# Residual sum ahead of the second norm: two fused operations on VectorE in place of one on ScalarE and two on GpSimd

## The reference

```
x = x + tanh(g_xattn) * _L0_xattn_ref(_layernorm(x), ctx, ctx, ..., ln_scale)
...
h = einsum('hst,htd->hsd', C / (normalizer + EPS), vh)          # inside _L0_xattn_ref
return (h - mu) / sqrt(var + LN_EPS) * ln_scale
...
x = x + tanh(g_ffn) * _L0_ffn_ref(_layernorm(x), w1, w2, w3, ..., gate_weight, ...)
```

## Time and profile before

| | before |
|---|---|
| median of 3 runs | 826.05 us (825.72 to 828.82) |
| the profiled execution | 823.55 us, span of the profile 821.5 us |
| TensorE / VectorE busy | 686.1 us (84%) / 544.9 us (66%) |
| ScalarE / GpSimd busy | 374.5 us (46%) / 403.2 us (49%) |
| mean granted TensorE clock | 0.803 of full speed; near half of it in the attention stage |

### The profile page before, as it was taken

How to read it: one execution, slowest core, us unless ns; L and a number is a source line. 1 busy time by engine, 2 the same in 40 slices (tenths; PEclk the granted TensorE clock), 3 DMA queues, 4 the chain that set the end, 5 groups by cost and what they waited for, 6 DMA issues and landing times.

```text
span 821.5 us, 17825 instructions
## 1 busy us (share of the span) xinstructions
PE 686.1 (84%) x6004; PEld 546.3 (66%) x6004; DVE 544.9 (66%) x1493; ACT 374.5 (46%) x940; POOL 403.2 (49%) x370
## 2 busy tenths in 40 slices
PE   1973888997897987214899999999999999999993
PEld 1532454664655656103799898898989989899893
DVE  8726888978978878695556565555655555555562
ACT  4335465666666566124444444343434444444441
POOL 5025488688687786002044444344353453534523
PEclk9995655555555555555999999999999999999997
DMA  9722887877877752036279779798897977969752
GB/s 287 245 92 60 265 259 223 281 233 235 262 234 251 244 185 83 27 78 261 87 222 290 240 229 325 205 296 246 240 308 221 278 256 229 324 199 283 254 159 52
DMA packets 85817, 179.70 MB, mean 219 GB/s; under 512 B 14881, under 2 KB 48546, under 8 KB 85730
## 3 DMA queue, kind: packets, MB, share of 16 engines
q1 hardware_dynamic: 63202, 140.10, 52.7%
q0 software_dynamic: 13824, 18.43, 10.3%
q10 hardware_dynamic: 8704, 20.06, 6.6%
HBM read 140.93 MB, written 38.67 MB: 219 GB/s over the span
## 4 chain that ended last, share of the span: by engine, by line
PE 50%; POOL 16%; DVE 12%; issue 11%; DMA 7%; ACT 2%; POOLq 0%; DVEq 0%; ACTq 0%
PE bank L1049 40%; POOL whl L467 8%; DMA out<-res,TS 5%; POOL x L700 2%; POOL qE L558 2%; POOL vp L542 2%; PE bank L301 2%; PE bank L304 2%; PE bank L1043 1%; POOL kw L550 1%; DMA w_d<-whl 1%; PE bank L505 1%; POOL vp L540 1%; DVE R L944 1%; PE bank L314 1%
## 5 line engine op out<-in xcount | busy, mean ns | idle before, releaser
L1049 PE MATMUL bank<-xh,w 128*128 128x256 bf16 (+1 forms) x1760 | 268.5, 263 | 9.8 <-DVE xl L1105 9.8
L1049 PE MATMUL bank<-xl,w 128*128 128x256 bf16 (+1 forms) x880 | 222.7, 263 | 0.0
L1031 POOL DMA_INDIRECT out<-res,TS x72 | 116.0, 1611 | 213.0 <-DVE res L1166 142.5
L1122 ACT ACTIVATE sg<-bank 128x256 f32<-128x256 f32 (+1 forms) x240 | 86.8, 362 | 230.4 <-PE bank L1049 230.4
L1049 PEld LDWEIGHTS bank<-xh,w 128*128 128x128 bf16 x1760 | 165.8, 98 | 28.8 <-issue 12.1
L1152 DVE TENSOR_TENSOR hf<-sg,bank 128x256 f32<-128x256 f32 (+1 forms) x200 | 78.9, 395 | 117.6 <-ACT sg L1122 117.6
L1049 PE MATMUL bank<-w,hh 128*128 128x256 bf16 x864 | 140.0, 273 | 0.0
L1022 POOL DMA_INDIRECT xg<-y_d,TG x72 | 72.5, 1006 | 86.1 <-DVE TS L979 53.0
L467 POOL TENSOR_TENSOR whl<-wst,whl 128x1224 bf16<-128x1224 f32 x32 | 80.0, 2501 | 44.9 <-ACT whl L455 44.9
L1049 PE MATMUL bank<-w,hlo 128*128 128x256 bf16 x360 | 98.1, 273 | 0.0
L1116 ACT CAST hh<-hf 128x256 bf16<-128x256 f32 (+1 forms) x240 | 90.3, 376 | 12.5 <-DVE hf L1154 12.5
(11 more groups left out here) (215 smaller groups left out, 1151.6 us busy)
## 6 DMA issues: line engine op xcount, KB each, us to landing
w<-w_d SPq DMA_DIRECT2D x40, 1408.0 KB, 9.2
w<-w_d SPq DMA_DIRECT2D x40, 768.0 KB, 4.7
wst<-in_wts SPq DMA_DIRECT2D x32, 612.0 KB, 4.2
w_d<-whl ACTq DMA_DIRECT2D x32, 612.0 KB, 5.6
vb<-in_kv SPq DMA_DIRECT2D x8, 528.0 KB, 5.7
xa<-in_x SPq DMA_DIRECT2D x8, 512.0 KB, 8.2
kT<-in_kv SPq DMA_DIRECT2D x8, 512.0 KB, 8.8
xc<-in_x SPq DMA_DIRECT2D x8, 512.0 KB, 5.2
```

The costliest lines, as they stand in the source:

```text
L1031: nc.gpsimd.indirect_dma_start(out, bass.IndirectOffsetOnAxis(ap=TS[:, c0:c0 + 1], axis=0), res[w][:, j, :], None, bounds_check=TOK - 1, o ...
L1049: mm = nc.tensor.matmul(dst, l, r, start=(n == 0), stop=(n == len(pairs) - 1))
L1122: nc.scalar.activation(sg[m % 2][0:K, 0:N], bank[0:K, 2 + (NM * w + m) % 4, 0:N], ACT.Silu).then_inc(f_sg, 1)
```

## The change

The first step leaves ScalarE (`c_hn_act` with L665) and the other two leave GpSimd (`c_pool` with L700 and L703). A new function does the same on VectorE, in slot t for tile t-1, between nb (L658) and the statistics of h. Its first operation is (h - mean) * lsg, its second (that) * rs + x; both are `scalar_tensor_tensor` on 128x256 fp32, with both tensor operands in SBUF and a per-partition scalar. The second waits for the first. The wait of ScalarE's rs step for the earlier tile names the finished x2 in place of its first step.

```diff
-        def c_hn_act(act, t):
-            c = t % NC
-            ge(act, c_nb, t + 1)
-            ge(act, c_y, t - 3)
-            ge(act, c_x2o[c], 16 * (t // NC))
-            nc.scalar.activation(x2[:, c, :], h[:, c, :], ACT.Identity, bias=nb[:, c, 0:1], scale=rs[:, c, 0:1]).then_inc(c_xn, 1)
+        def c_x2_dve(dve, t):
+            V = nc.vector
+            b, c = t // NC, t % NC
+            ge(dve, c_rs, t + 1)
+            ge(dve, c_mv2, t + 1)
+            ge(dve, c_y, t - 3)
+            ge(dve, c_x2o[c], 16 * b)
+            V.scalar_tensor_tensor(x2[:, c, :], h[:, c, :], mv[:, c, 0, 0:1], lsg[:, :], ALU.subtract, ALU.mult).then_inc(c_xn, 1)
+            ge(dve, c_xn, t + 1)
+            ge(dve, c_x[b % 2], 16 * (b // 2) + 16)
+            V.scalar_tensor_tensor(x2[:, c, :], x2[:, c, :], rs[:, c, 0:1], xc[b % 2][:, c, :], ALU.mult, ALU.add).then_inc(c_x2, 1)
...
-            ge(act, c_xn, t - 3)
+            ge(act, c_x2, t - 3)
...
-        def c_pool(pool, t):
-            G = nc.gpsimd
-            b, c = t // NC, t % NC
-            ge(pool, c_xn, t + 1)
-            G.tensor_tensor(x2[:, c, :], x2[:, c, :], lsg[:, :], ALU.mult).then_inc(c_xa, 1)
-            ge(pool, c_xa, t + 1)
-            ge(pool, c_x[b % 2], 16 * (b // 2) + 16)
-            G.tensor_tensor(x2[:, c, :], x2[:, c, :], xc[b % 2][:, c, :], ALU.add).then_inc(c_x2, 1)
...
-            if 0 <= t - 1 < NT:
-                c_hn_act(act, t - 1)
...
             if 0 <= t - 1 < NT + 2:
                 c_nb_dve(dve, t - 1)
+            if 0 <= t - 1 < NT:
+                c_x2_dve(dve, t - 1)
             if 0 <= t < NT:
                 c_sth_dve(dve, t)
...
-            if 0 <= t - 1 < NT:
-                c_pool(pool, t - 1)
```

More of the change, by code:

```diff
@@ L168, in build @@
         c_x = [sem(f"c_x{w}") for w in range(2)]; c_st2 = sem("c_st2"); c_mv2 = sem("c_mv2"); c_st3 = sem("c_st3"); c_mv3 = sem("c_mv3")
-        c_nb = sem("c_nb"); c_lv = sem("c_lv"); c_rs = sem("c_rs"); c_xa = sem("c_xa"); c_xn = sem("c_xn"); c_x2 = sem("c_x2"); c_y = sem("c_y"); c_yT = sem("c_yT"); c_yc = sem("c_yc")
+        c_nb = sem("c_nb"); c_lv = sem("c_lv"); c_rs = sem("c_rs"); c_xn = sem("c_xn"); c_x2 = sem("c_x2"); c_y = sem("c_y"); c_yT = sem("c_yT"); c_yc = sem("c_yc")
         c_lp = sem("c_lp"); c_lg = sem("c_lg"); c_x2o = [sem(f"c_x2o{c}") for c in range(NC)]; c_yo = [sem(f"c_yo{c}") for c in range(NC)]
```

## The result

The changed kernel takes 856.46 us (median of 4 runs, 854.84 to 857.25), against 827.33 for the kernel before in the runs beside it. The ratio is 1.036, with an interval from 1.034 to 1.038: 29 us slower. The profiled execution has a span of 852.7 us, 31.2 more than before. All of it arises in the attention stage: the first operation of the routing (zr) starts at 366.0 us in place of 334.9, the first transposes of the expert stage at 416.6 in place of 385.5.

The account below looks back on a forecast made before the run. VectorE, held up by GpSimd's weight split, was taken to bound the attention stage; 27 slots at 1.37 us gave 37.0, plus 1 for the rest, on 823.55: 861.6, as a median 864, rounded to 863 us, range 834 to 876.

Parts of the forecast that it names:

- the likeliest case: At Cl in each slot: weight split L467 starts 0.1 us ahead of Cl and holds it; 856 to 872 us, chance 0.45.
- Cl's first half gets in ahead: At Cl: its first half passes before split L467, which then holds the second half; 852 us, chance 0.2.
- VectorE is bound already and GpSimd holds it up: Attention stage before the change: of VectorE's 31.5 us batch, 22.0 work, 5.6 stalls beside GpSimd, 3.9 idle.
- The removed work counts for nothing: ScalarE loses 0.60 us and GpSimd 1.45 per slot; both costs hidden afterwards, nothing in the sum.
- x2 costs 0.9 per slot: The two new VectorE operations together add 0.8 to 1.0 us per slot, taken as 0.9, or 3.6 per batch.
- L467 starts 3.13 after Cm: On GpSimd, the weight split waits only for L455 and starts 3.13 us after Cm's start, before at 5.11.
- Cl then ends at +7.1: On VectorE, held by split L467, Cl lets the next operation start 7.1 us after Cm, undisturbed 4.44: 2.6 stall per slot.
- a lock taken strictly: At Cl: GpSimd's small operation between its halves paid in full, slot 0.3 us longer, sum some 8 us higher.
- The rest of the slot: From Cl's end to the next Cm: `b_h_dve` 1.45 us, plus 0.35 into D or 1.22 into A and B.
- The faster rival: GpSimd's chain was the true bound and split L467 finds a harmless place: 28.6 us per batch, 806 us, chance 0.12.

Follow-up runs that it names:

- the split first alone: Kernel before, with weight split L467 moved ahead of L700 and L703 in GpSimd's list, nothing else: 825.4 us, ratio 0.998.
- the last experiment: Kernel before, with Cl ahead of the statistics, split L467 ahead of L700 and L703 and waiting for Cl, L610 reading PSUM: 815.2 us, ratio 0.987.
- the doubled operation: Changed kernel, with the first of the two new VectorE operations issued twice, the extra one into a scratch tensor: 859.7 us, ratio 1.040.
- the best version: Changed kernel, with Cl ahead of the statistics, split L467 waiting for both halves of Cl, L610 reading PSUM: 804.1 us, ratio 0.973.
- the first reordered kernel: Changed kernel, with Cl (L577) moved ahead of the two statistics in VectorE's list, same operations: 824.1 us, ratio 0.996.

## Why the prediction was right

It said 863 us, range 834 to 876, slower with 0.8; measured 856.5. The number alone would not tell the likeliest case (856 to 872) from "Cl's first half gets in ahead" (852); the trace does, since the split (223.66) starts before Cl (223.80) and takes its undisturbed 2.50.

- *VectorE is bound already and GpSimd holds it up.* For the changed kernel it is shown: VectorE waits for no semaphore, and order alone takes back 32 us. For the kernel before it holds in part. That its waits count is shown by the step from the split first alone (825.4 us) to the last experiment (815.2), which changes VectorE's list, the split's wait and L610 and leaves all of GpSimd's work. But VectorE also waits for TensorE there, 3.9 us per batch, and in the last experiment still does; that it alone bound the kernel before is not shown.
- *The removed work counts for nothing.* GpSimd's busy share fell from 0.79 to 0.60 of the stretch and nothing was gained; it waits 59.7 us for L455 instead.
- *x2 costs 0.9 per slot.* 0.48 us each, 0.92 from the first one's start to the next operation. The lower of the two rows that it came from was misread: 0.39 is a mean over two shapes of L1138, and that of 128x256 alone is 0.42. But this term isn't what was paid, as the doubled operation shows. The wait absorbs it. Its effect was to put Cl behind the split, by 0.14 us; the prediction had 0.1. So narrow a margin, from a cost taken between two rows, was partly luck, as its chances said (0.45 against 0.2 for the next case); the sign did not hang on it. In the kernel before with the split first, Cl stands 0.9 earlier and passes in most slots.
- *L467 starts 3.13 after Cm.* 3.13.
- *Cl then ends at +7.1.* 7.12 in three slots of four, 7.23 in the slot into B. The likeliest of the three cases was the one that came. The 0.3 more per slot that the prediction gave for a lock taken strictly did not: from the split's end (226.16) to the end of Cl (227.73) it is 1.57 us, against 1.60 by its row.
- *The rest of the slot.* Here is the excess of 1.1 us per batch, times 6.75 batches 7.6 us, somewhat more than the whole distance from 863 to 856.5. I had `b_h_dve` at 1.45, from a slot where L610 had been drawn out to 0.45; after the change it is 1.17 or 1.31, because GpSimd has fewer small operations to put in front of it. And I had 0.25 for the L596 pair in A and B; it takes its undisturbed 0.62.
- *The faster rival*, a chain through GpSimd as the true bound: its sign was the wait before L700 and the chain's shares. In the kernel before, that chain stays in GpSimd's own list over most of a batch:

```profile
...
190.86 0.68 POOL vp L542
191.54 2.48 issue
...
194.07 0.72 POOL x L700
...
```

It puts down as "issue" the 2.48 us in which GpSimd waited for ScalarE's L665 (2.52 in the earlier trace rows), and a wait inside a VectorE duration has no part in it. So its shares did not say what set the time: the change took 5.8 of GpSimd's 24.8 us out of each batch, and nothing was gained. What the rival asked for, a harmless place for the split, exists, but takes a new order, and the changed kernel doesn't give it.

One point stays open: what would hold a batch below the 27.8 of the best version. TensorE is busy for 115 of 126 us there, VectorE for 121 and without a wait for a semaphore, so VectorE is the likelier limit still; no run takes the remaining waits out of its operations to show it.

## What to carry to other kernels

When work goes from one engine to another, ask what stood behind it on the engine that is relieved: it starts earlier now, and here that, and not the work itself, set the price. A duration that varied for one shape (0.14 and 1.45 us) was here a wait that no list of waits showed; find who was running, and count the operations of that kind that lie in the reach of the long one. Then set the order so that the long operation of GpSimd begins when VectorE works from PSUM or on statistics, and try a PSUM operand for the small ones that remain.

## What the hardware showed

- A VectorE operation of eight columns, SBUF to SBUF with one tensor input (L610), waits for a GpSimd operation just as one with two does: 2.39 us at most here. The same sum with a second operand from PSUM never did: 0.16 to 0.17 us, with a split in progress in each slot of a batch. But not every operation from SBUF to SBUF waits: the RECIPROCAL behind it, of the same eight columns, stayed at 0.20 beside the split (at 207.78 above), and the statistics (BATCH_NORM_STATS2, one SBUF input) at 0.39 to 0.43 throughout. The new form also changed the kind of the operation, from TENSOR_SCALAR to SCALAR_TENSOR_TENSOR; for the latter kind the operand decides, since nb (L658), with both in SBUF, waits. A TENSOR_SCALAR from PSUM beside a split was not run.
- A GpSimd operation gets in between two VectorE operations that stand one right behind the other, so that the second of a pair can be stopped when the first has passed: Cl at 201.09 in the first reordered kernel had started before the split and took 3.60 us.
- The wait is mutual. GpSimd's kw went from about 0.61 to 1.06 us, and the split from 2.50 to 2.86 or 2.95 where Cl was first.
- A scalar_tensor_tensor of 128x256 with a scalar per partition took 0.48 us, the tensor_tensor of the same size (L1138, this shape alone) 0.42.
- The Trainium skill ("SBUF — State Buffer", section "SBUF: two separate sides") describes one exclusive lock on the ports that VectorE and GpSimd share, taken by VectorE operations with two SBUF inputs or in a 2-port mode. The rows agree with it, for the two-input operations; that L610 was in such a mode no row here says.
